# A four-layer graph kernel: VectorE's loop branch ahead of the second aggregate copy, degrees summed tile by tile, second value halves between the first scores

## What is computed

```python
# layer 0: aggregate, then an MLP with an RMS norm (width 1024)
agg = epsilon * x + einsum('bnm,bmd->bnd', adj, x)
out = silu(rmsnorm(agg @ W1 + b1) * rms_weight) @ W2 + b2
# layer 1: sigmoid attention on the graph, normalised by its row sums
# layer 2: 8 heads; edges that are absent are masked
scores = q @ k.T / sqrt(32) + adj * W_e[h];  scores = where(adj != 0, scores, -inf)
out = (softmax(scores) @ v) @ W_o.T
# layer 3: graph convolution with the degrees
d = (adj.sum(-1) + 1e-5) ** -0.5
out = (d[:, None] * adj * d[None, :]) @ (x @ weight) + bias
```

## Time and profile before

| what | value |
|---|---|
| median of 3 runs | 3631.16 us (3631.14 to 3635.59) |
| the profiled execution, own time | 3630.93 us |
| its span, first to last instruction | 3629.1 us |
| granted TensorE clock, mean | 0.994 |
| one loop turn (1769.7 to 1879.5 us) | 109.8 us |

### The profile page before, as it was taken

One profiled execution on the slowest core, in us unless ns is written; L12 is line 12 of the kernel. 1 busy time (PEld: TensorE's weight loads), 2 busy tenths in 40 slices (PEclk: granted clock), 3 DMA queues, 4 the chain that ended last, 5 costly groups with the idle time before them and its releaser, 6 DMA issues.

```text
span 3629.1 us, 69233 instructions
## 1 busy us (share of the span) xinstructions
PE 3493.1 (96%) x19886; PEld 2540.7 (70%) x20108; DVE 2646.4 (73%) x6570; ACT 2291.2 (63%) x5062; POOL 851.8 (23%) x1995
## 2 busy tenths in 40 slices
PE   6999999999999999999999999999999999999997
PEld 4767677776777676777667777767776777777674
DVE  6777777777777777777777777777777777777764
ACT  4666666666676666666666766666666666666664
POOL 2122221222221222212222212222212222122220
PEclk8999999999999999999999999999999999999999
DMA  3233223232232332232322323322323223233212
GB/s 101 48 92 88 74 65 84 61 93 71 70 86 55 90 89 73 64 91 54 93 75 70 82 63 82 93 70 64 93 52 93 78 70 78 69 77 93 70 50 68
DMA packets 166941, 275.09 MB, mean 76 GB/s; under 512 B 23908, under 2 KB 59876, under 8 KB 166760
## 3 DMA queue, kind: packets, MB, share of 16 engines
q1 hardware_dynamic: 166760, 273.45, 28.4%
HBM read 122.37 MB, written 16.78 MB: 38 GB/s over the span
## 4 chain that ended last, share of the span: by engine, by line
PE 52%; issue 16%; DVE 12%; ACT 9%; POOL 6%; DMA 2%; SPq 2%; POOLq 0%; DVEq 0%; ACTq 0%
PE turn L1325 9%; PE value L1340 7%; PE score L1316 6%; PE front L1128 5%; PE front L1130 5%; PE front L1129 5%; PE front L1158 3%; PE score L1313 3%; DVE pT L899 3%; POOL small L402 3%; ACT prob L630 2%; POOL x_out L483 2%; DMA qk_stack<-qk 2%; PE front L1185 2%; DVE prob L975 2%
## 5 line engine op out<-in xcount | busy, mean ns | idle before, releaser
L630 ACT ACTIVATE prob<-prob,small 128x512 f32<-128x512 f32 x1024 | 736.6, 720 | 380.4 <-DVE small L975 376.9
L975 DVE CUSTOM_DVE_ANT_0 prob<-score,adj_sb,drv 128x512 f32<-128x512 f32 x1024 | 758.9, 746 | 127.0 <-PE score L1316 119.1
L1325 PE MATMUL turn<-ident,prob 128*128 128x128 f32 x4096 | 621.5, 274 | 33.9 <-ACT prob L630 32.9
L1316 PE MATMUL score<-qk_stack 128*128 128x512 f32 x1024 | 591.4, 581 | 10.4 <-DMA qk_stack<-qk 9.8
L1325 PEld LDWEIGHTS turn<-ident,prob 128*128 128x128 f32 x4096 | 482.8, 141 | 145.7 <-issue 63.4
L639 ACT ACTIVATE pT<-turn 128x512 f32<-128x512 f32 x768 | 449.2, 585 | 79.2 <-PE turn L1325 79.1
L1313 PE MATMUL score<-unlinked,neg_mask 128*128 128x512 bf16 x802 | 305.7, 381 | 14.0 <-DVE small L975 12.4
L738 DVE TENSOR_TENSOR s_lo<-front,s_hi 128x512 fp32r<-128x512 f32 x316 | 216.8, 686 | 129.5 <-ACT s_hi L531 129.3
L1128 PE MATMUL front<-w_hi,s_hi 128*128 128x256 f32 x1024 | 309.2, 302 | 0.1
L1130 PE MATMUL front<-w_hi,s_lo 128*128 128x256 f32 x1024 | 287.7, 281 | 0.0
L1129 PE MATMUL front<-w_lo,s_hi 128*128 128x256 f32 x1024 | 287.4, 281 | 0.0
(11 more groups left out here) (203 smaller groups left out, 7843.7 us busy)
## 6 DMA issues: line engine op xcount, KB each, us to landing
qk_stack<-qk SPq DMA_DIRECT2D x1024, 128.0 KB, 2.4
adjT_f<-in_adjT SPq DMA_DIRECT2D x32, 1024.0 KB, 5.3
adj_sb<-in_adj SPq DMA_DIRECT2D x32, 1024.0 KB, 7.5
prob<-in_adjT SPq DMA_DIRECT2D x32, 1024.0 KB, 5.4
x_new<-in_x SPq DMA_DIRECT2D x32, 512.0 KB, 4.9
out<-x_out SPq DMA_DIRECT2D x32, 512.0 KB, 3.0
pT<-in_W SPq DMA_DIRECT2D x2, 1024.0 KB, 11.0
rmsw_b<-in_rmsw SPq DMA_DIRECT2D x1, 512.0 KB
```

The source lines that it names most:

```text
L630: act.activation(prob[:, i % 8, :], prob[:, i % 8, :], ACT.Exp, bias=nmax[:, h, n:n + 1], scale=-1.0, accum_out=prsum[:, h, n:n + 1]).then ...
L975: dve.tensor_tensor_reduce(out=prob[:, i % 8, :], in0=SB_[i % 2][:, :], in1=adj_sb[:, n, :], scale=neg_w[:, h:h + 1], scalar=3e38, op0=ALU ...
L1316: pe.matmul(SB_[i % 2][:, :], qk_stack[:, h % 4, 0, tile(n)], qk_stack[:, h % 4, 1, :], start=False, stop=True).then_inc(sc_ps, 1)
L1325: last = pe.transpose(TB[k % 2][:, tile(n)], prob[:, (4 * h + n) % 8, tile(j)], ident[:, :])
```

## The change

1. VectorE's `aggregated(nx, 1)` and `restore_diagonal(nx)` leave the end of `phases` and become `next_aggregate(nx)`, which is called at the start of the loop body, after the branch, and once after the loop for the last graph. The order of VectorE's data instructions is the same; only the loop branch moves, from behind the copy to ahead of it.
2. The one reduction of 128x2048 behind `unlinked` becomes four of 128x512, one for each tile, at g = 8 to 11, behind that step's share of the MLP. GpSimd's `degrees(t)` goes from ahead of `hidden_norm(tf, 0)` to behind `hidden_norm(tf, 1)` and waits for all four.
3. On TensorE the first half of the second values leaves its place ahead of the scores and goes to g = -2 (ahead of the third scores), the second half goes from g = -2 to g = -1 (ahead of the fourth). ScalarE's copy `values(t, 1)` goes from behind the second exponential to behind the third.

```diff
@@ GpSimd @@
-                pool.wait_ge(deg_ready, at(t, 1, 1))
+                pool.wait_ge(deg_ready, at(t, 4, 4))
...
             def phases(t, tf, nx):
-                if t is not None:
-                    degrees(t)
                 if tf is not None:
                     hidden_norm(tf, 0)
                     hidden_norm(tf, 1)
                 if t is not None:
+                    degrees(t)
                     widen_inverse(t, 0)
@@ ScalarE @@
+                    if b and g == -1:
+                        values(t, 1)
                     if b and g + 4 < 4 * H:
                         exps(t, g + 4)
-                    if b and g == -3:
-                        values(t, 1)
@@ VectorE @@
-                dve.tensor_reduce(deg, adj_sb[:, :, :], AX.X, ALU.add).then_inc(deg_ready, 1)
+
+            def degree(n):
+                dve.tensor_reduce(deg[:, n:n + 1], adj_sb[:, n, :], AX.X, ALU.add).then_inc(deg_ready, 1)
...
+                    if b and 8 <= g < 12:
+                        degree(g - 8)
                     if b and g >= 0 and g % 4 == DVE_TURN:
                         turned_probs(t, g // 4)
...
-                if nx is not None:
-                    aggregated(nx, 1)
-                    restore_diagonal(nx)
+
+            def next_aggregate(nx):
+                aggregated(nx, 1)
+                restore_diagonal(nx)
...
+            next_aggregate(1)
             phases(0, 1, 2)
             with dve.Fori(1, B - 2) as t:
+                next_aggregate(t + 1)
                 phases(t, t + 1, t + 2)
+            next_aggregate(B - 1)
             phases(B - 2, B - 1, None)
@@ TensorE @@
-                if b:
-                    project_v(t, 1, (0,))
...
-                    if b and g == -2:
-                        project_v(t, 1, (1,))
+                    if b and g in (-2, -1):
+                        project_v(t, 1, (g + 2,))
                     if b and g < 0:
                         scores(t, g + 4)
```

## The result

| | median | lowest to highest | runs |
|---|---|---|---|
| before | 3631.57 us | 3631.14 to 3635.59 | 4 |
| after | 3662.3 us | 3660.75 to 3663.3 | 4 |

The ratio is 1.0082, 95% interval 1.007 to 1.0095. The profiled execution took 3660.75 us with a span of 3659.0, at the same mean granted clock of 0.994 as before. The kernel is 0.8% slower.

The account below looks back on a forecast made before the run. TensorE, busy 96% of the span, was taken as the bound, with waits at each graph's start. 3630.9 + 8.9 (parts 1 and 3) + 23.3 (part 2) = 3663 us, range 3620 to 3683.

Parts of the forecast that it names:

- The gain of 0.18 us a turn: Start of a loop turn: moving VectorE's branch brings TensorE's second q projection from +15.38 to +15.20 us behind L1174's product.
- the 0.07 us that the values' move was to gain: First scores: TensorE is ready 0.72 us earlier, but the stack of q and k lets only some 0.07 be gained.
- the 0.50: Fourth scores: the values' half moves them from 0.67 to 1.17 us behind the third, 0.50 later, all let through.
- The taken 0.60: Degrees on VectorE: each 128x512 reduction taken as 0.60 us, between 0.57 from below and 0.69 from above.
- The chain worked out for it: Reductions at g = 9 and 10 delay step 15's maximum, its exponential and g = 12's transposes: 0.75 us in 31 turns, +23.3.
- the branch's place: Sign on VectorE: the branch lies in the gap ahead of T_lo, covered with 1.5 us to spare.
- the fourth scores 0.2 to 0.3 later: Sign on TensorE: fourth scores come 0.2 to 0.3 us later behind L1174's product than before.
- the number of 31 new waits at g = 12: Sign on TensorE: transposes at g = 12 newly wait for the exponential, 0.7 to 0.8 us in 31 turns.
- The reductions are covered: Rival, chance 0.20: VectorE's idle time swallows the degree reductions, only parts 1 and 3 count, 3640 us.
- Faster: Rival, chance 0.18: stack lands 0.33 us earlier, the half fills TensorE's waits for VectorE, reductions are covered: 3621 us.
- Worse downstream: Rival, chance 0.12: ScalarE's backlog from g = 12 also delays g = 16's transposes, up to 0.6 us a turn: 3682 us.
- Stall stays: Rival, chance 0.05: the branch's stall stays on the path or shows again behind T_lo, +7 us on the forecast, 3670.

Follow-up runs that it names:

- e10: Kernel before with only VectorE's loop branch moved, plus two unused 128x1 memsets ahead of the loop to shift its code: 3625.55 us, ratio 0.9982.
- e1: Kernel before with only VectorE's loop branch moved ahead of the second aggregate copy: 3627.17 us, ratio 0.9989.
- e4: Kernel before with the loop branch and the second values moved, degrees left as one reduction: 3636.6 us, ratio 1.0016.
- e2: Kernel before with only the halves of the second values moved between the first scores: 3643.4 us, ratio 1.0032.
- e11: Kernel before with four degree reductions at g = 8, 9, 11 and 13, GpSimd's degrees ahead of widen_inverse(t, 1): 3654.76 us, ratio 1.0063.

## Why the prediction was right, and where not

The prediction was 3663, the measurement 3662.3. Both costs that make up the forecast were there and of the size said, so it was not right by chance; that the total is met to within 1 us is better than its steps were. By its steps:

**Part 1.** The gap ahead of T_lo covers the jump: 3.37 us of idle time stand there with it. The gain of 0.18 us a turn was read off one loop turn and the turn after the loop. Two things in that reading were off. The turn after the loop has the compare-and-branch too; it only falls through, and there are 28 jumps back, not 29. And the loop turn that was read has one of the shortest idle times behind the jump, 1.95 us of 1.95 to 2.23, so its first scores were at 5.66 where the mean is 5.75. The gain in e10 is 0.26 us a turn at the second q projection. Alone, in e1, the part gave only 15.48 - 15.35 = 0.13 us, because the biases then ran at 0.82. Nothing in the profile of before tells that. In after the spacing does not count, since TensorE's fourth scores come late: e4 has the slow spacing and after the fast one, and both are at 15.72. So there the whole gain stands against the cost of part 3.

The Trainium skill (Runtime: NRT & Kernel Launch, Instruction fetch mechanics) explains the cost of a taken branch by fetching the target's page. The traces agree in that the jump costs 2.70 us or more and the same branch falling through next to nothing; no run shows that it is a fetch. The Trainium skill's other figure, 0.108 us for a compare-and-branch (Advanced Engine Details and Errata, Control Flow Timing), is near the branch's own record, 0.060 to 0.068 us, and leaves out what follows a jump: by it alone e10 could not have gained 0.26 us a turn.

**Part 3.** The stack bounds the first scores, as forecast: 5.48 measured, 5.35 to 5.4 said. The fourth issue is at 3.07 in a loop turn instead of the 2.98 of the turn after the loop. And the 0.07 us that the values' move was to gain is not there: the first scores are at 5.48 with it (e4) and without it (e1). The forecast had the stack land 0.10 us ahead of the scores of the turn after the loop, by a transfer time of 2.36 us taken from a loop turn; that turn's own fourth transfer took 2.42 and landed 0.04 us ahead of them. Third to fourth scores is 1.17, exactly the sum made. That all of the 0.50 goes through is confirmed by e4 against e10, 15.72 - 15.22 = 0.50 at the second q projection, and by e2's +0.47. The values' copy did cost the q projection of g = 0, the new 21.1 us, and it ran beside the 0.50 as said: the projection comes 0.59 later (9.96 instead of 9.37), the second one 0.24. Start of a turn: forecast -0.18 - 0.07 + 0.50 = +0.25, measured -0.26 + 0 + 0.50 = +0.24. That the two gains add up to the same 0.25 is luck.

**Part 2.** The taken 0.60 is right as what a reduction costs its queue, and 0.68 is its duration. The Trainium skill (VectorE: DVE Perf Modes, The TRN2 errata) gave 0.69 for the duration, an estimate by its formula for the addition of two fp32 tensors; the row of 0.678 agrees. But instructions overlap by some 0.08, so the sum with 0.60 was the better one. Forecast for g = 12 was 0.75, measured 0.68, with 0.06 more by g = 13. The chain worked out for it ends as said: the step 15 bias 1926.61 + 0.75 = 1927.36, and the exponential starts at 1927.39. What that working did not see is the second way, through the step 14 bias and ScalarE's unbroken work, which is only 0.2 us shorter. So moving one of the two reductions away saves 0.2, not half, as e11 shows.

**The marks.** Right: the branch's place, the fourth scores 0.2 to 0.3 later, the second q projection (15.6 said, 15.72 measured), the number of 31 new waits at g = 12. Wrong in form: these waits show as 0.22 us each, not 0.7 to 0.8; the remaining 0.46 lies in the wait of `hidden(tf, 2, 0)` for s_lo and in products and weight loads that take longer without being called a wait. The loop turn is 111.65 instead of 110.71, while the forecast set 110.8 against a wrong 109.8; its difference of 1.0 is near the 0.94 measured.

**The rivals.** "The reductions are covered" fell: VectorE's 10.8 us of idle time lie elsewhere than at g = 9 and 10. "Faster" fell at the point named, the fourth scores, at 8.20 instead of before's 7.98. "Worse downstream" fell: the transposes of g = 13 to 31 all come 0.97 or 0.98 later, so nothing is added behind g = 13. "Stall stays" fell with the 5.48: the 2.7 to 3.0 us behind the jump are covered in every turn.

What stays open: why the code's place changes the spacing of the biases, and why the time behind a jump differs from turn to turn.

## What to carry to other kernels

Idle time of an engine in a stretch pays for nothing by itself: follow each added instruction to the engine that waits next, along every queue it delays, since taking away the last cause of a delay only leads to the second last. Work that is put between two dependent steps to fill a wait must be no longer than the wait: here 0.72 us of products filled 0.22. A wait that differs from turn to turn is to be read over many turns: here the one turn read, with 1.95 us, lay at the short end of 1.95 to 2.23, and the turn taken as the one without a branch had a branch that fell through. Where a gain of a few tenths of a microsecond per turn is at stake, time the edit also with its code shifted by an instruction or two, or the place of the code is measured in place of the edit.

## What the runs showed of the hardware that I had not expected

- VectorE's jump back to the loop's head left 2.70 to 3.06 us between the branch's record and the sequencer's next one, in each of 28 turns of thirteen kernels. Behind the same branch falling through the next data instruction waited 0.44 us for its input, no longer than in the turns without a branch ahead of it (0.46 and 0.54). The length differs from turn to turn, and where it is on the path the turn's length differs with it (first scores at 5.65 to 5.96 us in one execution).
- The distance of two like VectorE instructions in a loop body is 0.68 or 0.82 us depending on the number of instructions ahead of the loop: two more turned 0.82 to 0.68 in one kernel (0.9982 of the time before, where the unshifted has 0.9989) and 0.68 to 0.82 in the other (1.002). In the turns just ahead of and behind the loop it was 0.68 in all thirteen kernels.
- Four 128 KB transfers inside the chip, issued from two queues so that the last starts 0.6 us earlier, take longer: 2.82 us for the last instead of 2.36. The second to fourth land 0.64 to 0.74 us behind one another either way, so most of the earlier issue was lost.
- A 128x512 reduction lasts 0.678 us and takes 0.60 of its queue; the 128x2048 one takes 2.28, so cutting it in four costs next to nothing in VectorE's time. The cost was in where the quarters stand.
